# One core, adaLN attention and a mixture of experts: groups of experts set one further apart on TensorE

## The chip, the cores and the metric

The kernel runs on one core of a Trainium2 chip. The metric is the device time of one execution in microseconds; the median of three runs is given, with the lowest and the highest. A profile is one more execution, taken with the hardware profiler on; its times are us from the first instruction of the program.

## What is computed

A block with two halves over 1024 tokens of 256 numbers, all in float32. The first half is a layer norm, a modulation by vectors made from `c`, a second layer norm and causal attention. The change does not touch it. The second half is this, cut to what matters:

```python
h = layernorm(x) * (1 + cb) + sb
logits = h @ gate_w.T; scores = sigmoid(logits); sc = scores + gate_bias
# best 2 of 4 groups of experts, then the best K=4 of E=32 experts for each token
topk_w = 2.0 * scores[topk] / (scores[topk].sum(-1) + 1e-20)
slot = position of the token among those of its expert, kept if < CAP      # CAP = 64
buf[e, slot] = h[token]
hid = silu(buf @ w1[e]) * (buf @ w3[e])          # w1, w3: 256 x 128 for each expert
ob = hid @ w2[e]                                 # w2: 128 x 256
y[token] = sum over its 4 experts of topk_w * ob[e, slot]
out = x + gb * (y + silu(h @ shared_gate) * (h @ shared_up) @ shared_down)
```

## The kernel before, in words

The program is written by hand for each engine: every engine runs its own list of instructions in the order in which the source emits them, and semaphores tie the lists together. Nothing is scheduled by a tool. So an instruction that waits holds up all that stands behind it on its engine.

The routed part works on pairs of experts. A pair holds 128 rows, 64 slots of each of its two experts, and two pairs (four experts, 256 rows) make a **group** g, 0 to 7. One group goes through these steps, named as in the code:

- `gather(g)` (GpSimd, L497): two indirect DMAs fetch 128 rows each of 288 numbers from `token_rows` in HBM (L500). GpSimd starts them once `gather_idx` is made.
- `turn_slots(g)` (TensorE, L1611, matmuls of L1622): waits for both gathers, turns the rows by four 128x128 matmuls against the identity into banks 0 and 1. It also waits for the `slot_evac` of the group before, since there is one pair of banks.
- `slot_evac(g)` (ScalarE L741, VectorE L1153): one half each is copied out with the modulation, to `slotT`.
- `expert_up(g, r)` (TensorE, L1626, L1638): the products with w1 and w3 for pair r, four instructions for each r. In the trace every one of them shows twice, as float32 goes through in two passes.
- `expert_silu` (ScalarE, in before written in the loop, L762) and `expert_hid(g)` (VectorE, L1165): silu of one half times the other half.
- `turn_hid(g)` (TensorE, L1644, L1651) and `hid_evac(g)` (ScalarE, L750): the hidden rows are turned and copied to `hidT`.
- `expert_down(g)` (TensorE, L1654, L1660): the products with w2. `expert_evac(g)` (VectorE, L1174, L1181) scales both pairs into `ob`.
- `give_back(g)` (GpSimd, L505, L509): one indirect DMA for each pair scatters its rows to `results` in HBM, for the first 13 pairs (`BACK`). The last three pairs are not written out: they reach the sum by products with 0-or-1 maps on TensorE (`return_first`, `return_last`). `back_map` (L1185) makes the maps of the last two pairs, 16 instructions, and `back_map_first` (L1192) that of the pair before, 8 instructions, both on VectorE.

GpSimd's list is: gathers of groups 0 to 5, gather 6, `give_back(0)`, gather 7, `give_back(1)`, and then the others. Four `ob` buffers are used in turn.

The order of TensorE is written out in a loop (L1665 on), as are those of ScalarE and VectorE:

```python
turn_slots(0); shared_down(1, (0,))
for g in range(EGROUPS - 1):
    expert_up(g, 0)
    if g >= 1: turn_hid(g - 1)
    turn_slots(g + 1)
    expert_up(g, 1)
    if g >= 1: expert_down(g - 1)
    else: shared_down(1, (1,))
```

After the last group SyncE, which has waited for all 13 scatters, loads the returned rows of the eight token tiles (`yin`, L417 to L425), VectorE and TensorE add them (`add_rank` L1244, `add_ranks` L1251 to L1256, `add_sums` L1262, on TensorE L1710), and each tile is stored.

Of the kernel before, what the change touches and what calls it, by code (L numbers as in the profile page):

```python
# [39 lines left out]
def adaln_attention_moe(nc, x, qkv, o_proj, gamma, beta, gate_w, gate_bias, w1, w2, w3,  # L40
# [5 lines left out]
    NT = N // P  # L46
# [20 lines left out]
    with ExitStack() as ctx:  # L67
# [93 lines left out]
        back_first = w13_sb[:, 16].rearrange("p w k f -> p (w k f)").bitcast(BF16).rearrange("p (t q) -> p t q", t=NT)  # L161
# [363 lines left out]
        def _(act):  # L525
# [227 lines left out]
            slot_evac(0)  # L753
            for g in range(EGROUPS):
                if g >= 1:
                    hid_evac(g - 1)
                if g + 1 < EGROUPS:
                    slot_evac(g + 1)
                act.wait_ge(up_mm, g + 1)
                if g >= 2:  # L760
                    act.wait_ge(hid_done, g - 1)
                a.activation(act_h[:, g % 2], bank[4 + g % 2][:, :].rearrange("p (r w f) -> p r w f", r=2, w=2)[:, :, 0, :],  # L762
                             ACT.Silu).then_inc(silu_done, 1)
            act.wait_ge(ob_done, BACK + 1)
# [10 lines left out]
        def _(dve):  # L775
# [373 lines left out]
            shared_hid(1, 0)  # L1149
            shared_hid(1, 1)  # L1150
            shared_add(0)
# [58 lines left out]

            slot_evac(0)
            for g in range(EGROUPS - 1):
                slot_evac(g + 1)
                if g == 0:
                    shared_add(1)
                expert_hid(g)
                scores_of_slots(g)
                if g == 0:
                    score_sums()
                else:  # L1220
                    expert_evac(g - 1)
                if 1 <= g < 5:
                    back_map(2 * g - 2)
                    back_map(2 * g - 1)
                elif g >= 5:
                    for i in range(4 * g - 20, 4 * g - 16):
                        back_map_first(i)
            scores_of_slots(EGROUPS - 1)
# [53 lines left out]
        def _(pe):  # L1282
# [383 lines left out]
            shared_down(1, (0,))  # L1666
            for g in range(EGROUPS - 1):
                expert_up(g, 0)
                if g >= 1:
                    turn_hid(g - 1)  # L1670
                turn_slots(g + 1)
                expert_up(g, 1)
                if g >= 1:
                    expert_down(g - 1)
                else:
                    shared_down(1, (1,))
            last_g = EGROUPS - 1
            turn_hid(last_g - 1)
            expert_up(last_g, 0)
# [78 lines left out]
```

## Time and profile before

| what | value |
|---|---|
| median of 3 runs | 151.42 us |
| lowest, highest | 151.39, 151.52 us |
| span of the profiled execution, first to last instruction | 161.2 us |
| mean granted TensorE clock | 0.979 |
| TensorE matmul busy | 145.7 us (90%) |
| VectorE busy | 111.7 us (69%) |
| ScalarE busy | 65.0 us (40%) |
| GpSimd busy | 48.5 us (30%) |

The time of the profiled execution by the metric is not shown beside its span; the span alone is 9.8 us longer than the median of the executions without the profiler. An engine's busy time is an average over the whole kernel: the stages before 92 us are the same in both kernels, and what a change in the expert stage is worth must be read from the rows of that stage. "Idle before" is the idle time of an engine before an instruction, and the name behind the arrow is what ended it; "remote" there stands for an update that the trace cannot tie to an instruction that had just ended.

### The profile page before, as it was taken

Reading aid. Unit: us, or ns where it says so; the run is one execution under the profiler, and the core shown is the slowest. Engines: PE = TensorE matmul, PEld = TensorE weight load, DVE = VectorE, ACT = ScalarE, POOL = GpSimd, SP = SyncE. Lnnn points to the kernel's source line nnn. Section 1 sums busy time; section 2 is a strip of 40 time slices with the busy share of each in tenths; the row PEclk is TensorE's granted clock in tenths of the full one; section 3 lists DMA queues with packets and bytes.
Section 4 is the critical chain, followed back from the end, with each engine's and each line's share of the span. In section 5 each row is a group of like instructions: output and inputs, shape, how many; then the busy total and the mean of one; then the engine's idle time right before and its main releaser. Section 6 shows DMA issues by size and latency. Waiting matters only on the chain.

```text
span 161.2 us, 2747 instructions
## 1 busy us (share of the span) xinstructions
PE 145.7 (90%) x915; PEld 105.2 (65%) x915; DVE 111.7 (69%) x394; ACT 65.0 (40%) x173; POOL 48.5 (30%) x71
## 2 busy tenths in 40 slices
PE   7889799999999999999999999717997989699992
PEld 7846548468566775898787887404564555368881
DVE  2848989898986497798759824107672949559994
ACT  3233680486155428749879411101232323131000
POOL 7400004279520000002000077773176536500000
PEclk9999999999999999999999999995699999999999
DMA  4999999999999997001003034543014011159983
GB/s 114 277 385 387 418 418 375 349 348 348 352 348 350 347 349 242 1 28 51 0 5 109 2 76 117 116 116 94 0 47 105 33 48 45 47 151 343 406 283 134
DMA packets 22080, 31.28 MB, mean 194 GB/s; under 512 B 2065, under 2 KB 18231, under 8 KB 22066
## 3 DMA queue, kind: packets, MB, share of 16 engines
q1 hardware_dynamic: 20642, 27.71, 50.6%
q0 software_dynamic: 1424, 3.39, 7.8%
q8 instruction: 7, 0.11, 0.3%
q14 instruction: 7, 0.06, 0.1%
HBM read 23.65 MB, written 8.13 MB: 197 GB/s over the span
## 4 chain that ended last, share of the span: by engine, by line
PE 51%; DVE 26%; issue 7%; another core or an unknown queue 5%; DMA 4%; ACT 4%; SPq 1%; DVEq 0%
PE bank L1638 8%; PE bank L1445 7%; PE score_pair L1497 5%; PE bank L1660 4%; PE score_pair L1423 4%; PE score_pair L1419 4%; DMA w_sb<-in_L_wmod_dram 4%; PE bank L1497 3%; PE bank L1432 2%; PE score_pair L1445 2%; DVE base L1262 2%; PE score_pair L1651 2%; DVE aT L853 2%; PE score_pair L1295 2%
## 5 line engine op out<-in xcount | busy, mean ns | idle before, releaser
L1638 PE MATMUL bank<-w_sb,arena 128*64 128x256 f32 x128 | 18.3, 408 | 1.3 <-issue 1.2
L500 POOL DMA_INDIRECT arena<-token_rows,gather_idx x16 | 16.1, 1009 | 10.3 <-DVE gather_idx L1046 5.8
L509 POOL DMA_INDIRECT results<-arena,res_idx x11 | 11.0, 999 | 13.3 <-DVE arena L1181 10.9
L1445 PE MATMUL bank<-arena 128*128 128x256 f32 x56 | 13.7, 382 | 0.2 <-ACT arena L602 0.2
L1638 PEld LDWEIGHTS bank<-w_sb,arena 128*64 128x64 f32 x128 | 9.0, 145 | 7.5 <-issue 5.2
L473 POOL TENSOR_TENSOR base<-aT,mod 128x256 f32<-128x256 f32 x8 | 5.8, 726 | 24.3 <-DVE aT L857 20.6
L1445 PEld LDWEIGHTS bank<-arena 128*128 128x128 f32 x56 | 10.1, 190 | 2.3 <-issue 1.3
L593 ACT ACTIVATE prob<-score_pair,nmax 128x128 f32<-128x128 f32 (+7 forms) x8 | 5.9, 742 | 11.6 <-DVE nmax L930 11.5
L1651 PE MATMUL score_pair<-ident,h2T 128*128 128x128 f32 x16 | 3.7, 319 | 7.5 <-DVE base L1063 4.3
L1423 PE MATMUL score_pair<-arena 128*128 128x512 f32 (+3 forms) x24 | 10.1, 504 | 0.0
L1419 PE MATMUL score_pair<-arena 128*128 128x512 f32 (+3 forms) x24 | 9.8, 490 | 0.0
L750 ACT COPY prob<-score_pair 128x256 f32<-128x256 f32 x8 | 3.0, 372 | 16.3 <-PE score_pair L1651 9.9
L1660 PE MATMUL bank<-w_sb,prob 128*64 128x256 f32 x64 | 9.2, 412 | 0.0
L1651 PEld LDWEIGHTS score_pair<-ident,h2T 128*128 128x128 f32 x16 | 1.7, 149 | 10.9 <-issue 7.5
L743 ACT ACTIVATE arena<-score_pair,modc 128x256 f32<-128x256 f32 x8 | 4.5, 565 | 10.3 <-issue 5.0
L1155 DVE TENSOR_SCALAR arena<-score_pair,modc 128x256 f32<-128x256 f32 x8 | 4.3, 542 | 6.2 <-remote 4.4
L488 POOL DMA_INDIRECT first_row<-results,first_idx x1 | 1.2, 1247 | 23.6 <-DVE rows L956 23.6
L1170 DVE TENSOR_TENSOR h2T<-h2T,bank 128x256 f32<-128x256 f32 x8 | 3.3, 418 | 6.7 <-ACT h2T L762 3.7
L629 ACT ACTIVATE h2T<-bank,modc 128x128 f32<-128x128 f32 x16 | 6.3, 449 | 4.0 <-PE bank L1453 3.9
L1295 PE MATMUL score_pair<-arena,w_sb 128*128 128x512 f32 x16 | 7.3, 597 | 0.3 <-issue 0.3
L1295 PE MATMUL bank<-arena 128*128 128x256 f32 x32 | 7.5, 382 | 0.0
L1308 PE MATMUL score_pair<-ones_bf 128*128 128x128 bf16 x72 | 6.5, 278 | 1.1 <-POOL ones_bf L433 1.1
(223 smaller groups left out, 345.4 us busy)
## 6 DMA issues: line engine op xcount, KB each, us to landing
w_sb<-in_L_ffn_w_dram SPq DMA_DIRECT2D x12, 1024.0 KB, 12.5
results<-prob SPq DMA_DIRECT2D x1, 4096.0 KB, 15.8
w_sb<-results SPq DMA_DIRECT2D x6, 512.0 KB, 7.9
token_rows<-rows SPq DMA_DIRECT2D x8, 144.0 KB
xin<-in_L_attn_x_dram SPq DMA_DIRECT2D x4, 256.0 KB, 6.4
w_sb<-in_L_wmod_dram SPq DMA_DIRECT2D x1, 1024.0 KB, 9.5
out_dram<-base SPq DMA_DIRECT2D x8, 128.0 KB, 2.3
w_sb<-in_L_attn_qkv_dram SPq DMA_DIRECT2D x1, 768.0 KB, 7.6
```

The lines of the kernel that those rows point to most:

```text
L500: nc.gpsimd.indirect_dma_start(out=slot_in[:, r, :], out_offset=None, in_=rows_d, in_offset=bass.IndirectOffsetOnAxis(ap=gather_idx[:, r:r ...
L509: nc.gpsimd.indirect_dma_start(out=results_d, out_offset=bass.IndirectOffsetOnAxis(ap=res_idx[:, r:r + 1], axis=0), in_=ob[g % 4][:, (r % ...
L629: last = a.activation(h2T[:, k, P * i:P * i + P], ring_bank(f"x{i}")[:, P * k:P * k + P], ACT.Identity, bias=modc[:, 1, k:k + 1], scale=mo ...
L1295: last = t.matmul(dst, lhsT, rhs, start=(n == 0), stop=(n == len(terms) - 1))
L1308: t.matmul(bank[1][:, 0:P], ones_bf[:, :], ones_bf[:, :], start=True, stop=True)
L1419: t.matmul(dst[:, 0:w], qT[:, 0, P * i:P * i + P], xnT[:, 0, 512 * b:512 * b + w], start=True, stop=False)
L1423: last = t.matmul(dst[:, 0:w], qT[:, 1, P * i:P * i + P], xnT[:, 1, 512 * b:512 * b + w], start=False, stop=True)
L1445: last = t.matmul(PV_BANK[i][:, 0:H], probT[:, i % 2, j, :], vo[:, j, :], start=(j == 0), stop=(j == i))
L1497: last = t.matmul(SH_BANK[key][:, 256 * c:256 * c + 256], w[:, k, P * ft:P * ft + P], h2T[:, k, 512 * half + 256 * c:512 * half + 256 * c ...
L1638: last = t.matmul(bank[4 + g % 2][CAP * side:CAP * side + CAP, 2 * F * r:2 * F * r + 2 * F], slotT[:, k, CAP * e:CAP * e + CAP], w13_sb[:, ...
L1651: last = t.transpose(bank[2 + g % 2][:, P * r:P * r + P], hid[:, g % 2, r, :], ident[:, :])
L1660: last = t.matmul(bank[6 + g % 2][CAP * side:CAP * side + CAP, H * r:H * r + H], hidT[:, g % 2, r, CAP * side:CAP * side + CAP], w2_sb[:, ...
```

## The change

On TensorE `turn_slots` runs two groups ahead of `expert_up` where it ran one ahead, both halves of `expert_up` stand together, and `expert_down` follows two groups behind where it followed one behind; `turn_hid` stays one behind, and comes after both halves of the next `expert_up`. ScalarE and VectorE get lists to match. On VectorE the 16 `back_map` instructions leave the loop and go between the shared expert's steps ahead of it; the 8 of `back_map_first` go into iteration 1, and their target moves from a part of `w13_sb`, which is in use until group 4 is through, to a part of `xin`. The number of instructions that compute is the same. Nothing changes on GpSimd's list. The diff (line numbers are those of before on the left):

```diff
-        back_first = w13_sb[:, 16].rearrange("p w k f -> p (w k f)").bitcast(BF16).rearrange("p (t q) -> p t q", t=NT)
+        back_first = xin[:, 6:8, :].rearrange("p a b -> p (a b)").bitcast(BF16).rearrange("p (t q) -> p t q", t=NT)
@@ ScalarE
-            slot_evac(0)
-            for g in range(EGROUPS):
-                if g >= 1:
-                    hid_evac(g - 1)
-                if g + 1 < EGROUPS:
-                    slot_evac(g + 1)
...
+            def expert_silu(g):
                 act.wait_ge(up_mm, g + 1)
                 if g >= 2:
                     act.wait_ge(hid_done, g - 1)
...
+            slot_evac(0)
+            slot_evac(1)
+            for g in range(EGROUPS - 1):
+                expert_silu(g)
+                if g + 2 < EGROUPS:
+                    slot_evac(g + 2)
+                if g >= 1:
+                    hid_evac(g - 1)
+            hid_evac(EGROUPS - 2)
+            expert_silu(EGROUPS - 1)
@@ VectorE
-            shared_hid(1, 0)
-            shared_hid(1, 1)
-            shared_add(0)
+            settle()
+            shared_hid(1, 0)
+            for i in range(0, 2):
+                back_map(i)
+            shared_hid(1, 1)
+            for i in range(2, 4):
+                back_map(i)
+            shared_add(0)
             slot_evac(0)
+            for i in range(4, 6):
+                back_map(i)
+            slot_evac(1)
+            for i in range(6, NT):
+                back_map(i)
             for g in range(EGROUPS - 1):
-                slot_evac(g + 1)
+                expert_hid(g)
                 if g == 0:
                     shared_add(1)
-                expert_hid(g)
-                scores_of_slots(g)
+                if g + 2 < EGROUPS:
+                    slot_evac(g + 2)
+                if g >= 2:
+                    expert_evac(g - 2)
                 if g == 0:
                     score_sums()
-                else:
-                    expert_evac(g - 1)
-                if 1 <= g < 5:
-                    back_map(2 * g - 2)
-                    back_map(2 * g - 1)
-                elif g >= 5:
-                    for i in range(4 * g - 20, 4 * g - 16):
+                elif g == 1:
+                    for i in range(NT):
                         back_map_first(i)
-            scores_of_slots(EGROUPS - 1)
+                if g == 0:
+                    scores_of_slots(0)
+                scores_of_slots(g + 1)
+            expert_evac(EGROUPS - 3)
             expert_evac(EGROUPS - 2)
             expert_hid(EGROUPS - 1)
@@ TensorE
             turn_slots(0)
             shared_down(1, (0,))
+            turn_slots(1)
             for g in range(EGROUPS - 1):
                 expert_up(g, 0)
+                expert_up(g, 1)
+                if g == 0:
+                    shared_down(1, (1,))
+                if g + 2 < EGROUPS:
+                    turn_slots(g + 2)
+                if g >= 2:
+                    expert_down(g - 2)
                 if g >= 1:
                     turn_hid(g - 1)
-                turn_slots(g + 1)
-                expert_up(g, 1)
-                if g >= 1:
-                    expert_down(g - 1)
-                else:
-                    shared_down(1, (1,))
             last_g = EGROUPS - 1
+            expert_up(last_g, 0)
             turn_hid(last_g - 1)
-            expert_up(last_g, 0)
+            expert_down(last_g - 2)
             expert_down(last_g - 1)
             expert_up(last_g, 1)
```

TensorE at the start of the expert stage, before, from `turn_slots(0)` on (`score_pair0<-ident` is `turn_slots`, `w13_sb` is `expert_up`, `score_pair1<-ident` is `turn_hid`, `w2_sb` is `expert_down`, `shd_sb` the shared expert; banks 4 and 5 and banks 6 and 7 alternate by group):

```order
L1622 MATMUL score_pair0<-ident,arena 128x128 x4
L1295 MATMUL score_pair1<-shd_sb,aT 128x256 x2
L1638 MATMUL bank4<-w13_sb,arena 64x256 x4
L1622 MATMUL score_pair0<-ident,arena 128x128 x4
L1638 MATMUL bank4<-w13_sb,arena 64x256 x4
L1295 MATMUL score_pair1<-shd_sb,aT 128x256 x2
L1638 MATMUL bank5<-w13_sb,arena 64x256 x4
L1651 MATMUL score_pair1<-ident,h2T 128x128 x2
L1622 MATMUL score_pair0<-ident,arena 128x128 x4
L1638 MATMUL bank5<-w13_sb,arena 64x256 x4
L1660 MATMUL bank6<-w2_sb,prob 64x256 x4
```

The same place now (its line numbers are those of the changed kernel):

```order
L1638 MATMUL score_pair0<-ident,arena 128x128 x4
L1311 MATMUL score_pair1<-shd_sb,aT 128x256 x2
L1638 MATMUL score_pair0<-ident,arena 128x128 x4
L1654 MATMUL bank4<-w13_sb,arena 64x256 x8
L1311 MATMUL score_pair1<-shd_sb,aT 128x256 x2
L1638 MATMUL score_pair0<-ident,arena 128x128 x4
L1654 MATMUL bank5<-w13_sb,arena 64x256 x8
L1638 MATMUL score_pair0<-ident,arena 128x128 x4
L1667 MATMUL score_pair1<-ident,h2T 128x128 x2
L1654 MATMUL bank4<-w13_sb,arena 64x256 x8
L1638 MATMUL score_pair0<-ident,arena 128x128 x4
L1676 MATMUL bank6<-w2_sb,prob 64x256 x4
```

The second `turn_slots` stands ahead of the first `expert_up`, `turn_hid(0)` comes behind four halves of `expert_up` instead of three, and `expert_down(0)` behind six instead of four.

TensorE at the end of the stage, before, from `expert_down(5)` on:

```order
L1660 MATMUL bank7<-w2_sb,prob 64x256 x4
L1651 MATMUL score_pair1<-ident,h2T 128x128 x2
L1638 MATMUL bank5<-w13_sb,arena 64x256 x4
L1660 MATMUL bank6<-w2_sb,prob 64x256 x4
L1638 MATMUL bank5<-w13_sb,arena 64x256 x4
L1295 MATMUL score_pair0<-shd_sb,aT 128x256 x2
L1651 MATMUL score_pair1<-ident,h2T 128x128 x2
L1295 MATMUL score_pair0<-shd_sb,aT 128x256 x2
L1660 MATMUL bank7<-w2_sb,prob 64x256 x4
```

And now, from `expert_down(4)` on:

```order
L1676 MATMUL bank6<-w2_sb,prob 64x256 x4
L1667 MATMUL score_pair1<-ident,h2T 128x128 x2
L1654 MATMUL bank5<-w13_sb,arena 64x256 x4
L1667 MATMUL score_pair1<-ident,h2T 128x128 x2
L1676 MATMUL bank7<-w2_sb,prob 64x256 x4
L1676 MATMUL bank6<-w2_sb,prob 64x256 x4
L1654 MATMUL bank5<-w13_sb,arena 64x256 x4
L1311 MATMUL score_pair0<-shd_sb,aT 128x256 x2
L1667 MATMUL score_pair1<-ident,h2T 128x128 x2
L1311 MATMUL score_pair0<-shd_sb,aT 128x256 x2
L1676 MATMUL bank7<-w2_sb,prob 64x256 x4
```

`expert_down(5)` (bank7) and `expert_down(6)` (bank6) stand side by side now, without an `expert_up` or a `turn_hid` between them.

VectorE in iterations 1 and 2 of its loop now (`h2T` is `expert_hid`, `modc` is `slot_evac`, `slot_score,mod` is `expert_evac`):

```order
L1173 TENSOR_TENSOR h2T<-h2T,bank5 128x256
L1158 TENSOR_SCALAR arena<-score_pair0,modc 128x256
L1197 TENSOR_SCALAR xin<-count_f,slot_token 128x128 x8
L1165 COPY slot_score<-arena 64x2 x2
L1173 TENSOR_TENSOR h2T<-h2T,bank4 128x256
L1158 TENSOR_SCALAR arena<-score_pair0,modc 128x256
L1184 SCALAR_TENSOR_TENSOR arena<-bank6,slot_score,mod 128x256 x2
```

The eight `back_map_first` stand between `slot_evac(3)` and `expert_hid(2)`; ahead of `expert_evac(0)` there come `expert_hid(2)` and `slot_evac(4)`.

## Rows read from the trace of the kernel before

**Rows 1.** Busy time by stretch; columns as its first line says.

```profile
core 0: us, PE busy (x) PEld busy (x) DVE busy (x) ACT busy (x) POOL busy (x), PEclk, DMA share, GB/s
...
108.40:115.20 6.80, 5.39 (x26) 3.31 (x28) 3.87 (x13) 1.22 (x3) 1.63 (x2) 0.50 0.25 68
```

**Rows 2.** TensorE in order of time: start us, us, what, idle before.

```profile
99.45 1.08 PE L1638 MATMUL bank<-w_sb,arena 128*64 128x256 f32 x8
100.47 0.66 PE L1622 MATMUL score_pair<-ident,arena 128*128 128x128 f32 x4
...
102.07 1.13 PE L1295 MATMUL score_pair<-shd_sb,aT 128*128 128x256 f32 x4
...
109.81 0.69 PE L1651 MATMUL score_pair<-ident,h2T 128*128 128x128 f32 x2 [4.33 <-DVE base L1063]
```

**Rows 3.** The same view of TensorE, groups 2 to 7.

```profile
115.96 0.44 PE L1651 MATMUL score_pair<-ident,h2T 128*128 128x128 f32 x2
116.23 0.60 PE L1622 MATMUL score_pair<-ident,arena 128*128 128x128 f32 x4
116.76 1.08 PE L1638 MATMUL bank<-w_sb,arena 128*64 128x256 f32 x8
117.67 1.03 PE L1660 MATMUL bank<-w_sb,prob 128*64 128x256 f32 x8
118.54 1.03 PE L1638 MATMUL bank<-w_sb,arena 128*64 128x256 f32 x8
119.50 0.44 PE L1651 MATMUL score_pair<-ident,h2T 128*128 128x128 f32 x2
...
132.39 0.44 PE L1651 MATMUL score_pair<-ident,h2T 128*128 128x128 f32 x2 [0.58 <-DVE h2T L1170]
...
140.86 0.44 PE L1651 MATMUL score_pair<-ident,h2T 128*128 128x128 f32 x2 [1.39 <-DVE h2T L1170]
```

**Rows 4.** VectorE in order of time, the same columns.

```profile
103.71 0.54 DVE L1155 TENSOR_SCALAR arena<-score_pair,modc 128x256 f32<-128x256 f32 x1 [4.40 <-remote]
108.73 0.69 DVE L1063 TENSOR_TENSOR base<-score_pair,base 128x512 f32<-128x512 f32 x1 [4.48 <-remote]
109.34 0.41 DVE L1170 TENSOR_TENSOR h2T<-h2T,bank 128x256 f32<-128x256 f32 x1
...
110.05 0.43 DVE L1016 TENSOR_TENSOR xin<-mask_bf,rows 128x256 f32<-128x256 bf16 x1
...
111.17 0.20 DVE L1019 RECIPROCAL scale<-ssum 128x8 f32<-128x8 f32 x1
```

**Rows 5.** ScalarE in order of time.

```profile
106.60 0.38 ACT L762 ACTIVATE h2T<-bank 128x256 f32<-128x256 f32 x1 [2.33 <-remote]
```

**Rows 6.** GpSimd in order of time.

```profile
92.39 1.00 POOL L500 DMA_INDIRECT arena<-token_rows,gather_idx  x1 [5.75 <-DVE gather_idx L1046]
...
109.33 1.00 POOL L500 DMA_INDIRECT arena<-token_rows,gather_idx  x1 [0.30 <-issue]
116.29 1.07 POOL L509 DMA_INDIRECT results<-arena,res_idx  x1 [5.96 <-DVE arena L1181]
...
139.25 0.98 POOL L509 DMA_INDIRECT results<-arena,res_idx  x1 [0.65 <-DVE arena L1181]
```

**Rows 7.** DMA by stretch (last two columns share and GB/s), after the fourteenth gather.

```profile
112.00:112.50 0.50, 0.50 (x4) 0.24 (x2) 0.09 (x1) 0.15 (x1) 0.00 (x0) 0.50 0.05 9
```

**Rows 8.** SyncE in order of time, the loads of the returned rows.

```profile
141.80 0.32 SPq L422 DMA_DIRECT2D w_sb<-results  x1
```

**Rows 9.** VectorE by line, 112 to 140 us: count, busy us, mean ns.

```profile
L1181 DVE SCALAR_TENSOR_TENSOR arena<-bank,slot_score,mod 128x256 f32<-128x256 f32 x12 | 5.3, 480 | 2.3 <-PE bank L1660 1.5 <-remote 0.4
L1188 DVE TENSOR_SCALAR xin<-count_f,slot_token 128x128 bf16<-128x128 f32 x16 | 3.7, 298 | 0.0
...
L1194 DVE TENSOR_SCALAR w_sb<-count_f,slot_token 128x128 bf16<-128x128 f32 x8 | 2.0, 315 | 0.0
```

**Rows 10.** VectorE in order of time, the first of the final additions.

```profile
146.77 1.00 DVE L1244 SCALAR_TENSOR_TENSOR base<-w_sb,scale,base 128x256 f32<-128x256 f32 x2
```

## The prediction

> **What bounds the kernel now.** I read the busy time by stretch first, then TensorE in order of time, then who consumes its results, and last GpSimd and the final loads. A difference of 0.2% (0.3 us) is about what a measurement of this kernel can tell from no change.
>
> In the steady part of the expert stage TensorE has no gap. From one `turn_hid` to the next, 115.96 to 119.50, is 3.54 us [rows 3], and the pieces fill it: `turn_hid` 0.27 (115.96 to 116.23), `turn_slots` 0.53, half an `expert_up` 0.91 (116.76 to 117.67), `expert_down` 0.87, the other half 0.96. There a larger distance between a product and its use has nothing to hide.
>
> But the trace also has waits. `turn_hid(0)` follows 4.33 us of idle time [rows 2], the last `turn_hid` 1.39 [rows 3]. Between 119.50 and 132.39 three groups take 12.89 us, 2.27 more than three times 3.54 [rows 3]. The clock row shows the half level, 0.50, from 108.4 to 115.2, right behind the long idle time [rows 1]. These look like what the change is for: it puts more matmuls between `expert_up` and `turn_hid`.
>
> The question is what kind of waits they are. `turn_slots(1)` is recorded from 100.47 for 0.66 us [rows 2], so as ended at 101.13, yet VectorE copies its result only at 103.71 [rows 4]. `shared_down(1)` is recorded as ended at 103.20 [rows 2], and VectorE adds it at 108.73, after 4.48 us of waiting [rows 4]. ScalarE's first silu starts at 106.60 with the releaser "remote" [rows 5]. No instruction stands between; the signals of TensorE arrive 2.6 to 5.5 us behind the recorded ends. The Trainium skill (Perfetto Trace Analysis, Tensor Engine Instruction) says that a matmul's end in a profile is an estimate, and that the semaphore is updated once PSUM has acknowledged the bytes; by that page the engine may really have been late. The rows cannot tell that from an effect of profiling.
>
> The size tells. Without the late signals `turn_hid(0)` could run at about 104.3: `shared_down` ends at 103.2, its addition takes 0.61 until `expert_hid(0)` may start (108.73 to 109.34), that takes 0.41 [rows 2, 4]. So 109.81 is 5.5 us late. From there to 115.96 is 6.15, 2.6 over 3.54, which the half clock accounts for [rows 1 to 3]. With 2.3 and 1.4 from above the sum is 11.8 us, and the span of 161.2 would be 149.4. The median of the timed runs is 151.42, 9.8 below the profiled span, and a timed run has no less around it than the span holds. So the timed runs can have only a small part of these waits. I take it that they have almost none, and forecast from the trace without them.
>
> **What bounds it then** is GpSimd as much as TensorE. Its fourteen first gathers start from 92.39 to 109.33, 1.303 us apart [rows 6]. The last scatter is the 29th indirect DMA; with none waiting it starts at 92.39 + 28 x 1.303 = 128.9. In the trace it starts at 139.25 [rows 6]; less the delays ahead of it (5.5 + 2.6 + 2.3 = 10.4) that is 128.85. The two meet: GpSimd without its 5.96 us of idle time [rows 6] would work without a pause. SyncE's loads begin only after that scatter, 2.55 us after its start [rows 6, 8], while in the trace VectorE first takes a loaded tile at 146.77, 5 us after the first load was issued [rows 8, 10], since its own work was late by the 1.4 as well. Without the delays the end is 161.2 - 10.4 = 150.8 by the scatters and 149.4 by TensorE and VectorE, so the scatters decide; 150.8 leaves 0.6 to the median of 151.42 for what lies around the span.
>
> **The change, part by part.** Matmuls, copies and DMAs are the same in number and size, so nothing is removed; only waits move. Each part is set beside the kernel without the late signals:
>
> *`turn_slots(1)` ahead of `expert_up(0)`.* Before, `expert_up(0, 0)` began at 99.45 [rows 2] while the gathers of group 1 were under way. Now TensorE waits for them there. The second starts at 92.39 + 3 x 1.303 = 96.30. How long one takes to land: at least 2.55 (scatter to first load, [rows 6, 8]); at most 4.17, since `turn_slots(1)` ran at 100.47 [rows 2]. The nearest row: the fourteenth, started at 109.33, has DMA engines busy at a share of 0.05 at 112.0 to 112.5 and none later [rows 6, 7], so some 3.2, with its signal 3.3. That gives 99.6, 0.15 to 0.2 us of waiting. The Trainium skill (DMA: Bandwidth & Descriptors, Anatomy of one DMA — SWDGE) puts a DMA from GpSimd at 2.0 us and its bytes over 436e3 per us; an estimate by that page for 128 rows of 1152 bytes is 2.34 us, and TensorE would not wait at all, with a loss of 0.35 instead of the 0.6 below.
>
> *`expert_down(0)` two groups behind.* From 99.6 TensorE does four `turn_slots` (2.1), six halves of `expert_up` (5.5), half a `shared_down` (0.95), `turn_hid(0)` (0.27) and the product itself (0.87): 109.3. Before, it was behind 4 halves and 3 turns.
>
> *VectorE's order.* This is what decides when the first scatter may start. `shared_add(1)` ends at 103.75, `slot_evac(2)` at 104.3, `score_sums` takes 1.3 (110.05 to 111.37), four copies of scores 0.7 (`expert_hid` and two of them go from 109.34 to 110.05, [rows 4]): 106.3. Then `expert_hid(1)` 0.4, `slot_evac(3)` 0.5, the eight `back_map_first` 2.0 [rows 9], two copies 0.35, `expert_hid(2)` 0.4, `slot_evac(4)` 0.5: 110.45. The first half of `expert_evac(0)` takes 0.44 (two take 0.88; mean 0.480 with overlap, [rows 9]): 110.9. GpSimd starts 0.3 later, at 111.2. It is free at 92.39 + 14 x 1.303 = 110.6. So the scatters start **0.6 us late**, and as 15 indirect DMAs stand in line without slack, gather 7 and all scatters are late by as much.
>
> *The end of the stage.* `expert_down(5)` and `(6)` stand side by side. Three scatters (two of group 5, one of 6) follow within one product's time of 0.87, so the last starts at least 2 x 1.303 after the first of the three. `expert_down(6)` has the same work behind it as before. The first of the three is ready about 126.0 to 126.5, which puts the last at 129.0 to 129.4: no later than 128.9 + 0.6. It costs nothing more, but it would cost up to 1.7 (2 x 1.303 - 0.87) if GpSimd were otherwise ahead.
>
> *The 16 `back_map`.* They took 3.7 us in the loop [rows 9] and go where VectorE waits for the shared expert and for gathers, from 92 to 101 us. In the loop VectorE then has 0.9 us less in each of four groups, where TensorE did not wait for it. Gain zero, and zero cost if the idle places hold; if they do not, `slot_evac(1)` is late by at most two maps, 0.5 us.
>
> *Gather 7* lands at (92.39 + 17 x 1.303 + 0.6 + 3.3) = 118.4; `turn_slots(7)` now comes one group earlier, at about 118.3. It just fits; each 0.1 more of landing time is a wait of 0.2 there.
>
> Sum: 0.6 us on the chain of scatters, nothing on TensorE's. The forecast is 151.42 + 0.6 = **152.0 us**. Bounds of the unknown landing time: with 2.55 the loss is 0.35, with 4.17 it is 1.1 for `turn_slots(1)` and 0.8 more behind it, 1.9 in all.
>
> **Rivals.**
>
> 1. *The waits are in the timed runs too, and the change hides them* (faster). Between `expert_up` and its `turn_hid` there were 1.8 us of other matmuls (0.87 + 0.92) and are now 3.3 (0.53 + 0.87 + 1.84), more than the late signals of groups 2 to 7, at most 2 us. If all of 2.3 + 1.4 is there, the time is 151.42 - 3.7 + 0.6 = 148.3; if half is, 149.9, which I take for this case. For it: the idle time stands in the trace, and the page above describes late signals. Against it: the 9.8 us. It decides from 0.9 us of such waits on.
> 2. *The return has slack* (no change). If a gather lands in 2.55 us the loss is 0.35, and if the final additions on VectorE hold the end, none of it is seen: 151.5. In the trace they ran without pause behind the loads [rows 10].
> 3. *Gathers land late* (slower by more). At 4.17 us TensorE idles 1.1 us at `turn_slots(1)` and 0.9 at `turn_slots(7)`, behind gather 7, which stands in line behind `give_back(0)`: 153.3.
>
> **The numbers.** Forecast 0.39, rival 1 0.32, rival 2 0.19, rival 3 0.10. Faster by over 0.2%: 0.32; within: 0.19; slower: 0.49. The range is 149.3 to 152.9: it takes in rival 2, the nearer half of rival 1 and the forecast with its bounds up to 1.5 us of loss, and leaves out the full gain and the full rival 3, together less than 0.2. The cases of the likelier sign have 151.6 to 153.3.
>
> **What would show it.** In the profile of the changed kernel: `turn_slots(1)` starting within 0.3 us of 99.6 with TensorE idle ahead of it; the first scatter at 111 to 112 and the following fifteen 1.30 apart without idle time; VectorE's eight maps directly ahead of the `expert_hid(2)` that the first scatter's evacuation waits for; and late signals covered, so that its span may be several us shorter than 161.2 although the timed runs gain nothing. A span that falls with the timed median by like amounts, or timed runs under 151.1, would make my reading of the late signals wrong. GpSimd idle among the scatters would mean that TensorE sets their times, and then the side-by-side products cost more than I say.

## The result, and the profile after

| | before | after |
|---|---|---|
| median (lowest to highest, 4 runs each, taken together) | 151.47 us (151.39 to 151.63) | 153.23 us (152.87 to 153.55) |
| span of the profiled execution | 161.2 us | 151.8 us |
| its own time | not given | 153.55 us |
| its mean granted TensorE clock | 0.979 | 1.000 |

The ratio is 1.0099, 95% interval 1.0057 to 1.014: the change costs about 1.5 us (0.9 to 2.1; the medians differ by 1.76), where 0.6 was forecast, and the time is above the range of 149.3 to 152.9. The profiled span fell by 9.4 us while the timed runs rose.

TensorE of the changed kernel in order of time (start us, us, what, idle before):

```profile
99.23 0.63 PE L1638 MATMUL score_pair<-ident,arena 128*128 128x128 f32 x4
...
105.82 0.66 PE L1638 MATMUL score_pair<-ident,arena 128*128 128x128 f32 x4 [0.71 <-DMA arena<-token_rows,gather_idx]
...
109.09 1.08 PE L1676 MATMUL bank<-w_sb,prob 128*64 128x256 f32 x8
110.10 0.44 PE L1667 MATMUL score_pair<-ident,h2T 128*128 128x128 f32 x2
110.47 1.95 PE L1654 MATMUL bank<-w_sb,arena 128*64 128x256 f32 x16
112.35 0.66 PE L1638 MATMUL score_pair<-ident,arena 128*128 128x128 f32 x4
112.94 1.08 PE L1676 MATMUL bank<-w_sb,prob 128*64 128x256 f32 x8
113.95 0.44 PE L1667 MATMUL score_pair<-ident,h2T 128*128 128x128 f32 x2
114.32 1.95 PE L1654 MATMUL bank<-w_sb,arena 128*64 128x256 f32 x16
```

The long wait of [rows 2] is gone, and in these groups TensorE is busy without a gap. But from one `turn_hid` to the next (L1667, 110.10 to 113.95) it is now **3.85 us**, against 3.54 in [rows 3], for the same instructions. The pieces say where: `turn_hid` 0.37 (was 0.27), `expert_up` 1.88 (0.91 + 0.96), `turn_slots` 0.59 (0.53), `expert_down` 1.01 (0.87). The column before the operands' size is the tile of the array: 128\*128 for the turns, 128\*64 for `expert_up` and `expert_down`. Before, a group ran turn, turn, up, down, up: one change of tile shape and back. Now it runs turn, up, turn, down: two.

The weight loads (PEld, the same columns) show what differs at a change. First the kernel before, from its second profile, then the changed one:

```profile
109.04 0.63 PEld L1638 LDWEIGHTS bank<-w_sb,arena 128*64 128x64 f32 x8 [0.17 <-issue]
109.74 0.79 PEld L1660 LDWEIGHTS bank<-w_sb,prob 128*64 128x64 f32 x8
...
111.78 0.20 PEld L1651 LDWEIGHTS score_pair<-ident,h2T 128*128 128x128 f32 x2 [0.39 <-issue]
```

```profile
110.10 0.20 PEld L1667 LDWEIGHTS score_pair<-ident,h2T 128*128 128x128 f32 x2 [0.38 <-issue]
110.47 1.49 PEld L1654 LDWEIGHTS bank<-w_sb,arena 128*64 128x64 f32 x16 [0.17 <-issue]
112.35 0.42 PEld L1638 LDWEIGHTS score_pair<-ident,arena 128*128 128x128 f32 x4 [0.39 <-issue]
112.94 0.63 PEld L1676 LDWEIGHTS bank<-w_sb,prob 128*64 128x64 f32 x8 [0.17 <-issue]
```

Where the shape stays, the first weights of the next step are loaded ahead of its first product (`expert_down` of before: load at 109.74, product at 109.96). Where it changes, load and product start together, and the loads have paused for 0.17 us (to 128\*64) or 0.39 us (to 128\*128). Before, that happens twice in a group, now four times.

VectorE, then GpSimd, of the changed kernel, the same columns:

```profile
106.97 1.68 DVE L1197 TENSOR_SCALAR xin<-count_f,slot_token 128x128 bf16<-128x128 f32 x8
...
110.22 0.88 DVE L1184 SCALAR_TENSOR_TENSOR arena<-bank,slot_score,mod 128x256 f32<-128x256 f32 x2 [0.21 <-PE bank L1676]
```

```profile
92.16 1.00 POOL L500 DMA_INDIRECT arena<-token_rows,gather_idx  x1 [5.77 <-DVE gather_idx L1052]
...
101.34 1.00 POOL L500 DMA_INDIRECT arena<-token_rows,gather_idx  x1 [0.30 <-issue]
...
109.44 1.00 POOL L500 DMA_INDIRECT arena<-token_rows,gather_idx  x1 [0.31 <-issue]
111.50 1.02 POOL L509 DMA_INDIRECT results<-arena,res_idx  x1 [1.07 <-DVE arena L1184]
...
122.53 0.98 POOL L509 DMA_INDIRECT results<-aT,res_idx  x1 [0.81 <-DVE aT L1184]
...
125.64 0.98 POOL L509 DMA_INDIRECT results<-arena,res_idx  x1 [0.84 <-DVE arena L1184]
...
128.40 0.98 POOL L509 DMA_INDIRECT results<-arena,res_idx  x1 [0.49 <-DVE arena L1184]
...
130.98 0.98 POOL L509 DMA_INDIRECT results<-arena,res_idx  x1 [0.30 <-issue]
```

0.30 us of idle time before a DMA is GpSimd's own pace. What is above it is waiting for an evacuation: 0.77 ahead of the first scatter and 0.51, 0.54 and 0.19 ahead of three late ones. The last scatter starts 38.82 us after the first gather; 28 times 1.303 would be 36.5. SyncE's first load follows 2.55 us after it, as in [rows 6, 8]:

```profile
133.53 0.32 SPq L422 DMA_DIRECT2D w_sb<-results  x1
```

In the tables below "line" is the time from the first gather to the last scatter, and "waits" what GpSimd waited above 0.32 between DMAs in it, in the one profile of each kernel. Ratios are to the kernel before, measured beside it on the same chip.

### The profile page after: what moved, and what is told of

Its sections match the earlier page's. It is cut to its first block, busy times and chain, and to the rows that moved or that the text cites. A ratio compares the mean times of both kernels' runs of the same rounds, so it can differ in the third digit from the quotient of the medians.

```text
span 151.8 us, 2747 instructions
## 1 busy us (share of the span) xinstructions
PE 144.3 (95%) x915; PEld 103.5 (68%) x915; DVE 112.8 (74%) x394; ACT 65.1 (43%) x173; POOL 48.7 (32%) x71
## 4 chain that ended last, share of the span: by engine, by line
PE 50%; DVE 21%; DMA 12%; issue 5%; POOL 5%; ACT 3%; SPq 2%; POOLq 1%; DVEq 0%
PE bank L1461 7%; PE bank L1654 7%; PE score_pair L1513 5%; POOL arena L500 5%; PE score_pair L1439 4%; PE score_pair L1435 4%; PE bank L1676 4%; DMA w_sb<-in_L_wmod_dram 4%; DMA w_sb<-results 3%; DMA arena<-token_rows,gather_idx 3%; PE bank L1448 2%; PE score_pair L1461 2%; DVE base L1278 2%; PE score_pair L1638 2%; DVE aT L859 2%
## 5 line engine op out<-in xcount | busy, mean ns | idle before, releaser
L1654 PE MATMUL bank<-w_sb,arena 128*64 128x256 f32 x128 | 15.7, 385 | 0.0
L1654 PEld LDWEIGHTS bank<-w_sb,arena 128*64 128x64 f32 x128 | 8.5, 136 | 4.8 <-issue 1.3
L1676 PE MATMUL bank<-w_sb,prob 128*64 128x256 f32 x64 | 8.4, 389 | 0.0
L757 ACT ACTIVATE h2T<-bank 128x256 f32<-128x256 f32 x8 | 3.1, 383 | 12.4 <-PE bank L1654 12.4
L1324 PEld LDWEIGHTS score_pair<-ones_bf 128*128 128x128 bf16 x72 | 6.5, 135 | 1.1 <-POOL ones_bf L433 1.1
L935 DVE TENSOR_REDUCE bmax<-score_pair 128x1 f32<-128x128 f32 (+7 forms) x8 | 6.0, 751 | 1.7 <-PE score_pair L1439 1.7
L1184 DVE SCALAR_TENSOR_TENSOR arena<-bank,slot_score,mod 128x256 f32<-128x256 f32 x12 | 5.2, 479 | 2.5 <-PE bank L1676 2.4
```

What stands on the lines that cost most here:

```text
L935: chain(v.tensor_reduce(bmax[:, i:i + 1], score_pair[i % 2][:, 0:n], AX_X, ALU.max))
L1324: t.matmul(bank[1][:, 0:P], ones_bf[:, :], ones_bf[:, :], start=True, stop=True)
L1654: last = t.matmul(bank[4 + g % 2][CAP * side:CAP * side + CAP, 2 * F * r:2 * F * r + 2 * F], slotT[:, k, CAP * e:CAP * e + CAP], w13_sb[:, ...
L1676: last = t.matmul(bank[6 + g % 2][CAP * side:CAP * side + CAP, H * r:H * r + H], hidT[:, g % 2, r, CAP * side:CAP * side + CAP], w2_sb[:, ...
```

## The experiments

### The kernel before, profiled once more

No edit.

> The kernel before, profiled once more. If the late TensorE signals of the first profile (2.6 to 5.5 us behind the recorded ends, 4.33 us idle ahead of turn_hid(0)) belong to that one execution, they are absent here and the span is 149.4 to 150.8 us, as summed in the prediction, with every group 3.54 us long and the last scatter at about 128.9 us. If they belong to the kernel, the span is again near 161 us.

Span 150.8 us, own time 152.52; line 36.57, waits 0. TensorE, then GpSimd:

```profile
104.69 0.44 PE L1651 MATMUL score_pair<-ident,h2T 128*128 128x128 f32 x2
...
108.24 0.44 PE L1651 MATMUL score_pair<-ident,h2T 128*128 128x128 f32 x2
...
111.78 0.44 PE L1651 MATMUL score_pair<-ident,h2T 128*128 128x128 f32 x2
```

```profile
111.05 1.03 POOL L509 DMA_INDIRECT results<-arena,res_idx  x1 [0.30 <-issue]
...
129.34 1.18 POOL L509 DMA_INDIRECT results<-arena,res_idx  x1 [0.30 <-issue]
```

The 4.33, 1.39 and 5.96 us of [rows 2, 3, 6] are not there. They belonged to that one execution. The first `turn_hid` starts at 104.69 (the prediction had 104.3 for it), groups take 3.55, and the scatters run without a pause. So this is the profile to set that of the change against: the line is 2.25 us longer there (38.82), the first gather 0.61 earlier (92.16 against 92.77; it varies from 91.8 to 93.0 over the profiles, but for the one with additional work ahead of it), the first load 0.20 sooner behind the last scatter (2.55 against 2.75) and the rest from that load to the end 0.46 shorter (18.19 against 18.65). 2.25 - 0.61 - 0.20 - 0.46 = 0.98, the difference of the spans of 151.76 and 150.76 but for rounding.

### Shapes together, shapes apart, maps alone

**Theory S**: the additional change of tile shape lengthens the groups, and TensorE then sets the times of the scatters. Rivals: the later first scatter; the maps; the gathers. The first kernel is the changed one with the products in 128\*64 side by side (VectorE's two steps swapped to match; each `expert_down` also comes one `turn_slots` earlier):

```diff
-                if g + 2 < EGROUPS:
-                    turn_slots(g + 2)
                 if g >= 2:
                     expert_down(g - 2)
+                if g + 2 < EGROUPS:
+                    turn_slots(g + 2)
```

> The changed kernel with expert_down(g-2) moved ahead of turn_slots(g+2), so that in each group the products on 64 columns (expert_up, expert_down) stand together and those on 128 columns (turn_slots, turn_hid) stand together: one change of shape and back per group instead of two. Theory S (the loss is the second change of shape, 3.85 us per group in the changed kernel against 3.54 before): the groups fall to about 3.55 us, the last scatter starts about 1.5 us earlier and the time falls from 153.2 by 1.0 to 1.5 us, to 151.7 to 152.2. Theory D (the loss is the distance itself: downs two behind make the scatters late, with a wait for gathers at the start): the time stays within 0.3 us of 153.2.

The second is the kernel before, whose only edit takes the shapes apart:

```diff
-                turn_slots(g + 1)
                 expert_up(g, 1)
+                turn_slots(g + 1)
```

> The kernel before with turn_slots(g+1) moved from ahead of expert_up(g,1) to behind it, nothing else: no skew, but two changes of shape per group instead of one. Theory S: the groups take 3.85 us instead of 3.54, TensorE's part ends about 2 us later, and the time rises by 1.0 to 2.0 us from 151.5. Theory D: within 0.3 us of 151.5.

The third is the kernel before with VectorE's maps moved alone (`back_map` to the shared expert's steps, `back_map_first` to iterations 1 and 2).

> The kernel before with the VectorE part of the change alone: the 24 map instructions taken out of the later groups, 16 into the idle places ahead of the loop and 8 into iterations 1 and 2. Theory S and theory D both expect no difference beyond 0.3 us from 151.5, since TensorE did not wait for VectorE in the steady groups. If VectorE was the hidden bound of the kernel before, this is faster by 0.5 us or more. If the maps are what makes the changed kernel slow, it is slower by 1 us or more.

| kernel | ratio, 95% | group | line | waits |
|---|---|---|---|---|
| after, shapes together | 1.0027 (0.9995 to 1.0058) | 3.55 | 36.87 | 0 |
| before, shapes apart | 1.0091 (1.0059 to 1.0124) | 3.85 to 3.90 | 38.06 | 1.40 |
| before, maps moved | 0.9989 (0.9957 to 1.0021) | 3.55 | 36.66 | 0 |

TensorE of the first, one group (108.68 less 105.13, the `turn_hid` before it, is 3.55):

```profile
107.22 1.03 PE L1676 MATMUL bank<-w_sb,prob 128*64 128x256 f32 x8
108.18 0.66 PE L1638 MATMUL score_pair<-ident,arena 128*128 128x128 f32 x4
108.68 0.38 PE L1667 MATMUL score_pair<-ident,h2T 128*128 128x128 f32 x2
108.99 1.95 PE L1654 MATMUL bank<-w_sb,arena 128*64 128x256 f32 x16
110.77 1.03 PE L1676 MATMUL bank<-w_sb,prob 128*64 128x256 f32 x8
```

And of the second, then its GpSimd:

```profile
107.64 0.44 PE L1651 MATMUL score_pair<-ident,h2T 128*128 128x128 f32 x2
108.01 1.08 PE L1638 MATMUL bank<-w_sb,arena 128*64 128x256 f32 x8
109.03 0.66 PE L1622 MATMUL score_pair<-ident,arena 128*128 128x128 f32 x4
109.61 1.08 PE L1660 MATMUL bank<-w_sb,prob 128*64 128x256 f32 x8
110.53 1.03 PE L1638 MATMUL bank<-w_sb,arena 128*64 128x256 f32 x8
111.49 0.44 PE L1651 MATMUL score_pair<-ident,h2T 128*128 128x128 f32 x2
```

```profile
127.66 0.98 POOL L509 DMA_INDIRECT results<-arena,res_idx  x1 [1.63 <-DVE arena L1181]
```

Both directions agree. The old order with one more change of shape has the 3.85 us group and costs about as much as the whole change; the new order without it has 3.55. In the second kernel the first scatter is not late (18.3 us after the first gather, as before): its loss arises at the end of the row, where TensorE, 0.3 us slower in each group, has lost its lead over GpSimd. A rival falls with them: the two kinds of product also write to different banks, but a group goes from one bank, or pair of banks, to another five times in both versions of the old order and four times in both of the new. The maps cost and gain nothing that can be measured; this run has the eight of `back_map_first` in two parts, where the change has them in one, so the one place is not tested by itself.

### The cost of the change of shape by itself

The kernel before with additional products in the warm-up, of no use to the result: `wide` writes 128 columns, `narrow` 64, both over 256 elements in float32.

```diff
+            wide(8)
+            narrow(8)
+            for _ in range(4):
+                wide(2)
+                narrow(2)
+            wide(8)
+            narrow(8)
```

> The kernel before with a row of extra products in TensorE's warm-up, of no use to the result: 8 products on 128 columns, 8 on 64 columns (in pairs on the two halves), then four times 2 wide and 2 narrow in turn, then 8 wide and 8 narrow. The time as a whole means nothing here; the trace does. Theory S: the 16 products in alternation take longer than 8 wide and 8 narrow in a block, by 0.15 us for each change of shape and back beyond the first, so the four pairs by some 0.5 us (0.3 us for a pair if the cost is that of one group). If a change of shape costs nothing, the alternation takes the same as the block within 0.05 us.

TensorE (each product shows twice):

```profile
10.63 1.14 PE L1317 MATMUL score_pair<-ones_f 128*128 128x256 f32 x4
11.70 0.66 PE L1323 MATMUL score_pair<-ones_f 128*64 128x256 f32 x4
12.28 1.14 PE L1317 MATMUL score_pair<-ones_f 128*128 128x256 f32 x4
...
17.23 3.75 PE L1317 MATMUL score_pair<-ones_f 128*128 128x256 f32 x16
20.91 1.96 PE L1323 MATMUL score_pair<-ones_f 128*64 128x256 f32 x16
22.80 1.55 PE L1295 MATMUL score_pair<-w_sb,h2T 128*128 128x512 f32 x3
```

The same 8 wide and 8 narrow products take 6.60 us in alternation (10.63 to 17.23) and 5.57 in two blocks (17.23 to 22.80): 1.03 us for three more changes and back, **0.34 us each**, with no wait on another engine. In the kernels it is 3.85 - 3.55 = 0.30. The Trainium skill (TensorEngine Tiling (Array Packing), Key Properties) says that changing the tiling mode, and not just the tile, drains TensorE. It gives no price; the trace agrees in so far as there is one, and as the weight loads pause at each change. The prediction did not use this rule, which speaks against the change.

### Who sets the end: one scatter less

Both kernels without the scatter of pair 2, whose rows are missing in the sum (the counts of the waits lowered to match):

```diff
                 for r in range(2 * g, min(2 * g + 2, BACK)):
+                    if r == 2:
+                        continue
```

With them ran the changed kernel and the first kernel of the last section once more.

> The changed kernel itself, beside the kernel before and the next run on one chip. Slower than before by 0.8% to 1.4% (1.2 to 2.1 us) as in the result; theory S expects it 0.8 to 1.5 us above the version with the shapes together. GpSimd idle among the scatters, last scatter about 38.8 us after the first gather against 36.6 in the kernel before.

> The changed kernel with expert_down(g-2) ahead of turn_slots(g+2), again, now on one chip with the changed kernel. Theory S: within 0.3% of the kernel before, and 0.8 to 1.5 us below the changed kernel. Theory D (distance and the wait for gathers are the loss): within 0.3 us of the changed kernel.

> The kernel before without the scatter of pair 2 (its rows are not returned; nothing else is left out). Theory G (GpSimd's line of 29 indirect DMAs without a pause sets the end): the last scatter starts 1.3 us earlier and the time falls by 0.8 to 1.3 us. If the scatters had slack, the time stays within 0.3 us.

> The changed kernel without the scatter of pair 2 (its rows are not returned). Theory S says that here TensorE paces the later scatters: GpSimd was idle 0.81, 0.84 and 0.49 us ahead of scatters 6, 8 and 10, so the idle time grows and the last scatter starts where it did; the time stays within 0.4 us of the changed kernel. If GpSimd's line is the bound here too, it falls by 0.8 to 1.3 us.

| kernel | ratio, 95% | line | waits |
|---|---|---|---|
| after | 1.0080 (1.0045 to 1.0115) | 38.97 | 2.06 |
| after, one scatter less | 1.0093 (1.0052 to 1.0133) | 38.27 | 2.68 |
| before, one scatter less | 0.9953 (0.9918 to 0.9987) | 36.17 | 0.88 |
| after, shapes together | 1.0031 (0.9999 to 1.0063) | 37.80 | 1.11 |

Before, one DMA of 1.30 us less gains 0.7 us (0.2 to 1.2): GpSimd's line set the end. The gain is under the 0.8 to 1.3 expected, and in the profile the line is only 0.40 us shorter, since GpSimd then waits 1.20 us (0.30 of it its pace) ahead of the DMA at 126.23: TensorE is the next bound, 0.4 us behind. After, it gains nothing in time: GpSimd waits longer instead. Its line is 0.7 us shorter in that profile, but so is the way from the first gather to TensorE's last `turn_hid` (37.55 against 38.25).

A second reading says the same without the time. Set the last scatter against the last `turn_hid`, on TensorE. In the changed kernel it starts 0.72 us after it in both profiles, and 0.72 with one scatter less: a scatter taken away does not move it, TensorE sets it. Before, it starts 0.04 us ahead of it, and 0.43 ahead with one scatter less, which is as early as TensorE lets it. With the shapes apart it is 0.44 ahead: TensorE sets it there too. So the change has moved the bound of the return from GpSimd to TensorE, where only 0.4 us lay between the two.

The difference between the changed kernel and "shapes together" is smaller here than in the first table of experiments: the medians are 153.20 and 152.68, 0.5 us apart, where 0.8 to 1.5 was expected, and the ratios differ by 0.5% (0.7% there). In the repeat of "shapes together" `turn_slots(3)` waited 0.84 us for its gather, and the first scatter was 0.43 late. In the first profile neither happened. The repeat's groups were 3.55 us, and yet two late scatters waited, 0.55 and 0.18 above the pace.

### Two attempts at the rest

Shapes together is still 0.3% over before, at the edge of what can be told. Two kernels were to find that rest. One is the changed kernel with `turn_slots(1)` between the halves of `expert_up(0)`, and `turn_hid(0)` ahead of `turn_slots(3)`:

> The changed kernel with only the start of TensorE's order as before: turn_slots(1) between the halves of expert_up(0), turn_hid(0) ahead of turn_slots(3), the later groups as changed. It keeps the second change of shape. Theory S: still slower than before by 0.5% or more (1.0 us or so), since the wait for gathers (0.7 to 0.9 us at turn_slots(3)) is at most partly saved and the groups stay at 3.85 us. If the wait for gathers were the main loss, it is within 0.3% of before.

It gives 1.0105 (1.0064 to 1.0146), groups of 3.85, waits of 1.66 (in a profiled execution of 154.58 us, where the median was 153.79): no gain, so the order of the start is not where the loss of the change is. The other is "shapes together" with `expert_down(5)` moved from beside `expert_down(6)` to behind `expert_down(4)`, `turn_hid(5)` ahead of both, and halves of `shared_down` as cover:

> The skewed kernel with the shapes together, and at the end of the stage expert_down(5) moved up behind expert_down(4), apart from expert_down(6), with shared_down as cover in between. Of the 0.3% by which the version with the shapes together is still above before, this asks how much is the queue of three scatters at the end. If that is the rest of the loss: last scatter 36.6 to 36.9 us after the first gather and the time within 0.2% of before. If the rest is the wait for gathers at the start: still 0.3% above before. It cannot beat before by more than 0.2%, since GpSimd's line of 29 is without a pause there.

1.0054 (1.0028 to 1.0081), line 37.17, waits 0.34: not better than shapes together. It does not settle what the products side by side cost. The wait ahead of the scatters of group 5 is gone, but one of 0.36 above the pace stands ahead of those of group 4, whose product the edit puts behind `turn_hid(5)`, and TensorE has half a `shared_down` more to do ahead of the last `turn_hid`.

### Each half of the skew alone

The kernel before with `expert_down` two behind and nothing else (and VectorE's `expert_evac`):

```diff
                 expert_up(g, 1)
-                if g >= 1:
-                    expert_down(g - 1)
+                if g >= 2:
+                    expert_down(g - 2)
```

> The kernel before, with expert_down two groups behind turn_hid's group order (and VectorE's expert_evac to match) and nothing else: turn_slots stays one group ahead, each group has one change of tile shape and back. Theory S (changes of tile shape make the group longer): groups of 3.55 us from turn_hid to turn_hid as before, so none of the 0.8 to 1.0% of the change. For the 0.3 to 0.5% that is left when shapes stand together: if it comes from turn_slots waiting for gathers asked for earlier, this kernel has a ratio of 0.999 to 1.001, no wait of TensorE for a DMA at turn_slots, GpSimd idle under 0.4 us. If it comes from the later products and the two side by side at the end, the ratio is 1.003 to 1.005, the first scatter starts 18.6 us or more after the first gather (18.3 before), and GpSimd has an idle time of 0.5 us or more there or among the last four scatters. Rival to S (the longer distance between turn_hid and expert_down is what costs): ratio 1.008, groups 3.8.

1.0278 (1.0234 to 1.0323), more than anything expected, though nearer to the second of the two readings (later products) than to the first. The groups are 3.55, so the distance itself does not lengthen them. The loss is in three places. TensorE, GpSimd and SyncE, and TensorE's clock by stretch (PEclk is the third number from the right):

```profile
108.98 1.03 PE L1661 MATMUL bank<-w_sb,prob 128*64 128x256 f32 x8
...
144.27 2.77 PE L1712 MATMUL bank<-w_sb,ident 128*128 128x256 f32 x8 [2.89 <-DMA w_sb<-results]
```

```profile
111.70 1.07 POOL L509 DMA_INDIRECT results<-arena,res_idx  x1 [1.68 <-DVE arena L1181]
...
130.70 1.02 POOL L509 DMA_INDIRECT results<-arena,res_idx  x1 [0.30 <-issue]
```

```profile
134.85 0.32 SPq L422 DMA_DIRECT2D w_sb<-results  x1
```

```profile
146.00:148.00 2.00, 2.00 (x6) 1.33 (x5) 1.89 (x5) 0.00 (x0) 0.00 (x0) 0.50 1.01 354
```

First, `expert_down(0)` starts at 108.98, 2.57 later than the 106.41 of before, the first scatter is 1.38 late, another 0.59, and the line is 38.61. Second, the first load starts 4.15 us behind the last scatter instead of 2.55 to 2.75: that scatter took 4.0 us to land, where the same scatter takes 2.6 in the kernel before and 2.4 in the changed one. Why is open. Third, TensorE idles 2.89 us ahead of the final additions, and its granted clock is at the half level behind that (0.50 is 1.2 of 2.4 GHz). The half level itself does not show in the times: the one run with a mean clock of 0.999 took 155.63 us, the fastest of the five with 0.989 took 155.64. 2.0 + 1.5 + 0.6 for the slower end is 4.1, where 4.2 us were measured; the two profiled spans differ by 3.3 only, since the first gather starts 0.68 earlier in this one.

The kernel before with `turn_slots` two ahead and nothing else but `slot_evac(1)`, moved to the start with it on ScalarE and VectorE:

> The kernel before, with turn_slots two groups ahead (turn_slots(1) ahead of the first expert_up, turn_slots(g+2) where turn_slots(g+1) stood) and nothing else: expert_down stays one behind, each group has one change of tile shape and back. Theory S: groups of 3.55 us. If the 0.3 to 0.5% that is left comes from waits for gathers, the profile shows TensorE waiting 0.4 to 1.1 us for gather data at turn_slots(2) or turn_slots(3), and the ratio is 1.003 to 1.005, also where one profile happens to show no wait. If it comes from the later products and the end of the stage, the ratio is 0.999 to 1.001 and the last scatter starts 36.6 us after the first gather as before, since the scatters are GpSimd's own line even with a wait of TensorE of up to 0.9 us.

1.0684 (1.0632 to 1.0736), and it answers another question. Groups take 5.2 us, since TensorE waits at every turn:

```profile
108.17 0.63 PE L1625 MATMUL score_pair<-ident,arena 128*128 128x128 f32 x4 [2.00 <-DVE arena L1156]
```

`turn_slots(g+2)` stood where it needs the copy of the group before out of the one pair of banks, and ScalarE and VectorE make that copy behind other work. The later `slot_evac` have to be moved with it. The wait for a gather that was expected is there, 1.09 us of idle time at `turn_slots(2)`, but as a test of what it costs the kernel is of no use.

What the profiles show beside that: the skewed order without the additional shape changes has its first scatter on the edge. `expert_evac(0)` starts at 109.06 there and the scatter 1.27 later, at 110.33, exactly when GpSimd is free; before, it starts at 107.85 with GpSimd free at 111.05, so 1.9 us in hand. A gather that lands late, or a step later, is then seen at once (by 0.43 us in the repeat, by 1.38 with `expert_down` later still). The last scatter is on TensorE's edge too: it starts 0.76 and 0.72 us after the last `turn_hid` in the two profiles of "shapes together", where before TensorE allows it 0.43 ahead. That these two make the remaining 0.3% is argued from the profiles; no run shows it by itself.

## Why the prediction was wrong, point by point

**The late signals: right.** I took the waits of [rows 2 to 5] for something that the timed runs don't have, 149.4 to 150.8 for the true span. The second profile has 150.8. Rival 1 falls with it, and its 0.32 for a gain was too much for a case with 9.8 us against it. The span fell by 9.4 us though the timed runs gained nothing, as the prediction had it for this case.

**The bound: right, but by little.** Scatters without a pause, last one at 129.34 in that profile (128.9 forecast); one scatter less gains time before. But TensorE allowed the last scatter only 0.4 us sooner, a lead that the prediction did not work out.

**`turn_slots(1)`: too high by 0.2.** It ran at 99.23 without a wait, 3.17 us after its gather's start at 96.06. But gather 3, started at 101.34, let `turn_slots(3)` wait 0.71 until 105.82, 4.48 us later. I took one landing time for all; they differ by over a microsecond, and I looked only at the first and the last place.

**The first scatter: 0.6 forecast, 0.76 measured** (111.50 against 109.44 + 1.30), from terms that partly cancel. `expert_down(0)` ends 0.8 later than I had it (at 110.10, where it was to be 109.3; the wait at `turn_slots(3)` is in that), VectorE is 0.2 earlier (110.22 for 110.45), and from the start of the evacuation to the scatter it is 1.28, not 0.44 + 0.3. "This is what decides", said of VectorE's order, is wrong by a little: VectorE was through with it at 110.01 and idled 0.21 for TensorE's product.

**The step that failed** is the first sentence of the change's cost: "Matmuls, copies and DMAs are the same in number and size, so nothing is removed; only waits move", and its result, "nothing on TensorE's". The order of the same matmuls is itself a cost: 0.30 us in each group. TensorE takes 15.34 us for the four groups from 106.31 to 121.65 instead of 14.18 at 3.545. The rows were there: `turn_slots` behind `turn_hid` and `expert_down` behind `expert_up` had no transition between them in [rows 3]; and where half an `expert_up` stood between two turns, in [rows 2], it took 1.02 us (99.45 to 100.47) against 0.91 and 0.96 in [rows 3]. I costed each instruction by its duration in the old order, whatever stood beside it. By the runs this is the larger part: 0.8 to 1.0% with the shape changes, 0.3% without, which is some 0.7 to 1.1 us of the 1.2 to 1.5. What is left, 0.4 to 0.5 us, is near the 0.6 that the prediction had in all.

**The end of the stage: wrong by that.** "It costs nothing more" assumed GpSimd as the slower one there. The text named the sign, GpSimd idle among the scatters, and it appeared (0.51, 0.54, 0.19); but the reason given, the products side by side, is at most a small part of it: of these waits only the 0.19 stands ahead of a scatter of group 5, the first of the two. The slower groups are in the others, and so is the late start of TensorE behind `turn_slots(3)`, since the repeat of "shapes together" has such waits with groups of 3.55.

**The maps: right**, cost and gain zero in the run that moves them.

**A count that was off.** For rival 1 the prediction has 3.3 us of other matmuls between an `expert_up` and its `turn_hid` in the new order. It left out one `turn_slots`, one `expert_down` and the `turn_hid` before: in the trace of the changed kernel it is 5.45 us (`expert_up(2)` ends at 108.50, `turn_hid(2)` starts at 113.95). Nothing in the forecast hangs on it.

**Rival 3** gave 153.3, next to the 153.23 measured. That is chance for the most part: it took gathers landing at 4.17 for the cause at groups 1 and 7, and neither waited. One wait of its kind came, at group 3.

## What to carry to other kernels

When the order of matmuls is changed, write the tile shape beside each and count the changes before and after; the same instructions took 8% longer for it here (3.85 against 3.55 us). A step that is moved back by one place eats the lead of whatever consumes it: work out how much lead there is in a profile where nothing waits. A wait that stands in one profile only, and that the timed runs have no room for, is to be profiled again before a kernel is reordered to hide it.

## What was not expected of the hardware

- A change between 128-column and 64-column float32 products and back costs 0.34 us by itself and 0.30 in the kernel, at the full clock (granted 1.00 in these stretches).
- Gathers of one size, 1.30 us apart, did not land alike: one within 3.17 us of its start, one after some 4.4; a scatter's landing, mostly 2.1 to 2.8 us, was 4.0 once, for the one that the loads waited for.
- One profiled execution had TensorE's signals arrive 2.6 to 5.5 us behind the recorded ends; none of the other 14 profiles, one of them of the same kernel, shows such a thing, and its span was over 10 us longer than the second profile's.
- The first weight load behind a change of tile shape did not overlap the product ahead of it (idle 0.17 or 0.39 us), where loads for the same shape did.
